# The perceiver stage's next batch of rows loaded from another DMA queue, and one value projection a step earlier

## The reference

```python
xn = layernorm(x, ln_x_g, ln_x_b)
ln = layernorm(latents, ln_l_g, ln_l_b)
q = ln @ Wq
kv_input = jnp.concatenate((xn, ln), axis=1)
kv = kv_input @ Wkv
k, v = jnp.split(kv, 2, axis=-1)
...
sim = jnp.einsum('bhid,bhjd->bhij', q, k)
sim = jnp.where(mask_full[:, None, None, :], sim, max_neg)
attn = softmax(sim)
out = jnp.einsum('bhij,bhjd->bhid', attn, v)
```

## Time and profile before

| | |
|---|---|
| median of 3 runs | 3383.18 us (3382.89 to 3386.95) |
| the profiled execution, own time | 3382.07 us |
| its span | 3380.3 us |
| PE busy | 3005.5 us, 89% of the span |
| VectorE busy | 2083.6 us, 62% |
| ScalarE busy | 1558.0 us, 46% |
| GpSimd busy | 1327.4 us, 39% |
| mean granted clock of PE | 0.934 |
| moved by DMA | 220.43 MB, mean 65 GB/s |

### The profile page before, as it was taken

One profiled execution on the slowest core, in us unless ns is written; L12 is line 12 of the kernel. 1 busy time (PEld: TensorE's weight loads), 2 busy tenths in 40 slices (PEclk: granted clock), 3 DMA queues, 4 the chain that ended last, 5 costly groups with the idle time before them and its releaser, 6 DMA issues. The chain is left out here.

```text
span 3380.3 us, 44846 instructions
## 1 busy us (share of the span) xinstructions
PE 3005.5 (89%) x16620; PEld 2534.8 (75%) x16620; DVE 2083.6 (62%) x4123; ACT 1558.0 (46%) x3036; POOL 1327.4 (39%) x913
## 2 busy tenths in 40 slices
PE   6888999968664999999999999999999769999998
PEld 5677777744433898989899898989989657777777
DVE  4766666622365776767777676777767654444432
ACT  2333333311033676767667676766767522222222
POOL 1444444410021465656556565655656530111110
PEclk9899999977765999999999999999999979999999
DMA  5112121112078112121211112111121231111100
GB/s 178 36 46 60 48 61 39 48 66 95 3 267 318 46 34 61 36 61 37 62 37 34 59 37 62 37 59 35 36 62 37 79 127 35 68 50 50 50 25 25
DMA packets 131551, 220.43 MB, mean 65 GB/s; under 512 B 44750, under 2 KB 46799, under 8 KB 127246
## 3 DMA queue, kind: packets, MB, share of 16 engines
q1 hardware_dynamic: 117933, 168.09, 16.4%
q10 hardware_dynamic: 13408, 49.56, 4.0%
HBM read 112.01 MB, written 69.47 MB: 54 GB/s over the span
## 5 line engine op out<-in xcount | busy, mean ns | idle before, releaser
L1635 POOL TENSOR_SCALAR pa_Pr<-pa_Pr,pa_rs 128x590 f32<-128x590 f32 x512 | 904.6, 1771 | 699.9 <-DVE pa_rs L1864 699.9
L1868 DVE TENSOR_REDUCE pa_least<-pa_S 128x1 f32<-128x590 f32 x512 | 391.3, 764 | 242.3 <-PE pa_S L1699 240.4
L1764 ACT ACTIVATE pa_PTh<-pa_W 128x512 fp32r<-128x512 f32 (+1 forms) x640 | 367.7, 596 | 174.4 <-PE pa_W L1710 158.5
L1819 DVE TENSOR_TENSOR pa_PTl<-pa_W,pa_PTh 128x512 fp32r<-128x512 f32 (+1 forms) x640 | 422.0, 683 | 33.2 <-ACT pa_PTh L1764 25.4
L1796 ACT ACTIVATE pa_Pr<-pa_S,pa_least 128x590 f32<-128x590 f32 x512 | 385.2, 752 | 79.3 <-DVE pa_least L1868 76.2
L1710 PE MATMUL pa_W<-pa_ident,pa_Pr 128*128 128x128 f32 (+1 forms) x2560 | 368.7, 275 | 9.7 <-DVE pa_Ql L1834 8.9
L1710 PEld LDWEIGHTS pa_W<-pa_ident,pa_Pr 128*128 128x128 f32 (+1 forms) x2560 | 306.8, 143 | 34.0 <-DVE pa_Ql L1834 12.0
L1724 PE MATMUL pa_O<-pa_PTh,pa_V 128*128 128x512 f32 (+1 forms) x640 | 293.2, 458 | 11.6 <-DVE pa_PTl L1819 8.1
L1697 PE MATMUL pa_S<-pa_U,pa_Qh 128*128 128x296 f32 (+1 forms) x1024 | 234.1, 311 | 44.7 <-DMA pa_Um<-pa_U 44.4
L1725 PE MATMUL pa_O<-pa_PTl,pa_V 128*128 128x512 f32 (+1 forms) x640 | 257.8, 403 | 0.0
L1697 PEld LDWEIGHTS pa_S<-pa_U,pa_Qh 128*128 128x128 f32 x1024 | 180.3, 195 | 71.1 <-DMA pa_Um<-pa_U 47.7
(11 more groups left out here) (400 smaller groups left out, 7223.2 us busy)
## 6 DMA issues: line engine op xcount, KB each, us to landing
pa_Um<-pa_U SPq DMA_DIRECT2D x128, 147.5 KB
pa_Qh<-pa_Qh SPq DMA_DIRECT2D x128, 128.0 KB
o_s<-pa_O_pair SPq DMA_DIRECT2D x64, 256.0 KB, 2.6
ex_o_raw<-o_s SPq DMA_DIRECT2D x8, 2048.0 KB, 10.8
z_s<-la_z_hi ACTq DMA_DIRECT2D x8, 1180.0 KB, 7.6
z_s<-la_z_lo ACTq DMA_DIRECT2D x8, 1180.0 KB, 10.0
pa_z_hi<-z_s ACTq DMA_DIRECT2D x8, 1180.0 KB, 6.0
pa_z_lo<-z_s ACTq DMA_DIRECT2D x8, 1180.0 KB, 10.1
```

The lines of the kernel that those rows point to most:

```text
L1635: pool.tensor_scalar(p, p, rs[:, g % 2, t:t + 1], None, ALU.mult).then_inc(*pool_s.mark("probs", n))
L1764: act.activation(out, src, ACT.Copy, scale=scale).then_inc(*act_s.mark("hi", *name))
L1819: dve.tensor_tensor(out, src, f32(hi_ap), ALU.subtract).then_inc(*dve_s.mark(*name))
L1868: dve.tensor_reduce(least[:, g % 2, t:t + 1], scored[n % 2], AX, ALU.min).then_inc(*dve_s.mark("least", n))
```

## The change

The loads of `z` move from ScalarE's queue to SyncE's. For batch 0 they are issued between the second and the third slab of weights (`w_sync` is split); for a next batch right behind the two key copies of the last pair, ahead of the output store, and SyncE waits for the last keys' matmuls first (they are the last readers of the rows in `z`). ScalarE issues none. And for the first quad of a batch, the last value projection (j = 4) comes at tick 16 instead of 17.

```diff
--- before.py
+++ after.py
@@ -1551,7 +1551,7 @@
         for q in range(QUADS):
             base = 2 * LEAD * (q - 1)
             for j, (tick, early) in enumerate(((6, True), (7, False), (14, True), (14, False), (15, False)) if q % BQ else
-                                              ((13, True), (13, False), (14, False), (15, False), (17, False))):
+                                              ((13, True), (13, False), (14, False), (15, False), (16, False))):
                 v_at.setdefault((base + tick, early), []).append((q, j))
         v_unit = lambda q, j: ("V", q, j // 2 * 2)
         v_last = lambda j: j % 2 or j == NC - 1
@@ -1585,7 +1585,13 @@
         @block.sync
         def _(sp):
             sp.dma_start(mask_words[:, :], a["mask_BxS2_bk0"]).then_inc(mask_in, 16)
-            w_sync(sp)
+            def load(b):
+                for n in range(2):
+                    sp.dma_start(f32(z[n][:, :, :]), z_s[n][b:b + 1].rearrange("b p c z -> p (b c) z")).then_inc(z_in, 16)
+
+            w_sync(sp, 0, 2)
+            load(0)
+            w_sync(sp, 2)
             sp.wait_ge(mask_row, 1)
 
             def store(p):
@@ -1607,6 +1613,9 @@
                     r = slice(x * HD, (x + 1) * HD)
                     sp.wait_ge(*act_s.after("hi", "K", p, 1, x))
                     sp.dma_start(f32(Um[m][x][r, :]), f32(U[m][x][r, :])).then_inc(dup[m], 16)
+                if p % BP == BP - 1 and p + 1 < PAIRS:
+                    sp.wait_ge(*pe_s.after("K", p, 1))
+                    load(p // BP + 1)
                 if p >= 2:
                     store(p - 2)
             for p in range(PAIRS - 2, PAIRS):
@@ -1756,10 +1765,6 @@
 
         @block.scalar
         def _(act):
-            def load(b):
-                for n in range(2):
-                    act.dma_start(f32(z[n][:, :, :]), z_s[n][b:b + 1].rearrange("b p c z -> p (b c) z")).then_inc(z_in, 16)
-
             def copy(out, src, *name, scale=1.0):
                 act.activation(out, src, ACT.Copy, scale=scale).then_inc(*act_s.mark("hi", *name))
 
@@ -1787,7 +1792,6 @@
                         act.wait_ge(*pe_s.after("PV", *divmod(g * NC + c - RING, NC)))
                     copy(PTh[0:KEYS[c], ring(g, c), :], bank_of[u][0:KEYS[c], :], *u)
 
-            load(0)
             w_scalar(act, 0, FIRST)
             for n in range(1 - LEAD, STEPS + 2 * NT + 1):
                 g, t = divmod(n, NT)
@@ -1797,8 +1801,6 @@
                                    bias=least[:, g % 2, t:t + 1], accum_out=rs[:, g % 2, t:t + 1]).then_inc(*act_s.mark("exp", n))
                 for u in evacuated(n - 1):
                     read(u)
-                    if u[0] == "K" and u[2] == 1 and u[1] % BP == BP - 1 and u[1] + 1 < PAIRS:
-                        load(u[1] // BP + 1)
                 if n in (-4, -3, -2):
                     w_scalar(act, n + 7, n + 8)
                 if t == 0 and head(g - 2):
```

## The result

| | before | after |
|---|---|---|
| median | 3383.38 us (4 runs, 3382.89 to 3386.95) | 3327.14 us (4 runs, 3322.43 to 3332.2) |
| ratio, 95% interval | | 0.9832 (0.9814 to 0.985) |
| the profiled execution, own time / span | 3382.07 / 3380.3 us | 3332.2 / 3330.4 us |
| mean granted clock | 0.934 | 0.938 |

The change takes 56 us off; the forecast was 57, to 3325.

A forecast was written before the change was run, and what follows sets the result against it. PE's work was taken to set the perceiver stage's pace, so any PE idle time removed is gained. 48 + 5 + 4 = 57 us off 3382 gave 3325 us, range 3311 to 3346.

The forecast's parts named there:

- the three places: Batch changes, last value unit and stage's start, forecast to take 48, 5 and 4 us off, 57 in all.
- The copies before z: At seven batch changes, key copies issued ahead of z end PE's wait: 6.9 us each, 48 us (37 to 58).
- the rival that it is mostly clock: At the batch changes, from the experiments' theories: the first part's gain is mostly clock; no size or chance given.
- the clock too high: From scores to query at a batch change: 7.15 us against 4.26 at full clock, so low clock costs 2.9 us.
- the rival of the falling clock: At the batch changes the clock falls all the same: 2.9 us seven times, 20 us; 3345 us, chance 0.11.
- the first term: At seven batch changes: key copies issued before z, 48 us off (37 to 58).
- The value unit: Last value unit one step earlier, seven times: 0.6 us new wait for 1.28, 5 us off (0 to 8.9).
- The start: Stage's start: first weight slabs go before z, third slab is cut earlier; 4 us off (0 to 5.5).
- The store behind z: At batch changes VectorE's O write waits about 2 us longer; cost 0, without cover up to 10 us in all.
- Turns between the queues: At batch changes, packets of z still get among the copies', PE waits as before: 9 us left, 3373 us, chance 0.05.
- A queue that works off its DMAs one after the other: SyncE's queue at batch changes and start: each transfer waits for the one ahead; slower, 3398 us, chance 0.04.
- the rival asked for 2 us more: At the batch changes z comes 2 us later, the query waits, 14 us given back: 3339 us, chance 0.07.

The follow-up runs named there:

- e4: Kernel before with ScalarE still issuing the next batch's z loads, but later, behind SyncE's key copies: 3340.61 us against 3384.68, ratio 0.9869.
- e9: Changed kernel with the next batch's two z loads issued ahead of the key copies in SyncE's queue: 3371.18 us against 3382.7 for the kernel before, ratio 0.996.
- e6: Changed kernel run again, nothing altered: 3327.93 us against 3382.86 for the kernel before, ratio 0.9837.
- e12: Changed kernel with z loads in halves and each batch change's output store issued from ScalarE's queue: 3320.52 us against 3382.7 for the kernel before, ratio 0.9815.
- e10: Changed kernel with z loads issued later, after the scores that open the next pair: 3369.24 us against 3382.7 for the kernel before, ratio 0.996.
- e1: Kernel before with only the last value projection moved from tick 17 to 16: 3375.8 us against 3384.68, ratio 0.997.
- e11: Changed kernel with each batch change's output store issued from ScalarE's queue, just ahead of the copies: 3326.1 us against 3382.7 for the kernel before, ratio 0.9832.
- e7: Changed kernel with each z load cut in two halves, each with its own semaphore: 3323.15 us against 3382.86 for the kernel before, ratio 0.9824.
- e8: Changed kernel with each z load cut in four pieces of one chunk: 3336.57 us against 3382.86 for the kernel before, ratio 0.9858.
- e5: Changed kernel with the output store issued ahead of the two z loads in SyncE's queue: 3351.74 us against 3382.86 for the kernel before, ratio 0.9911.

## Why the prediction was right

The measured total is nearer to the forecast than its parts are: the three places give 54.5 us of 57 in the profiled executions; the nearly 2 us that the medians' 56 have beyond that are no more than scatter.

*The copies before z: forecast 48 us, measured 45.5.* The mechanism held in each step: the copies' wait went seven times of eight, PE ran on to the query, and a wait for z took its place (forecast 1.4 us each, measured 1.3). The interval was to be 22.5 us and is 22.9 on average. The forecast put the query 9.98 us behind the copies' issue (1280.1 - 1270.12), the first change has 10.67. PE was ready after 1279.11 - 1.71 - 1268.44 = 8.96 us, forecast 8.58. The pair e4 and e9 shows that order alone does this.

*How it divides.* The sums over the seven intervals across a change, before and in e6 (us in all, busy us of each engine, means):

```profile
sum 206.03, PE 160.74 PEld 141.85 DVE 123.62 ACT 111.37 POOL 98.91; mean PE 22.96 PEld 20.26 DVE 17.66 ACT 15.91 POOL 14.13
sum 157.92, PE 143.67 PEld 125.59 DVE 120.77 ACT 112.36 POOL 98.66; mean PE 20.52 PEld 17.94 DVE 17.25 ACT 16.05 POOL 14.09
```

PE's busy time falls by 17.1 us and its idle time by 31.0. So the gain is mostly idle time, and the rival that it is mostly clock fails. The forecast had put the clock too high, at 2.9 us a change; it is 2.4. What was off is the way from the scores to the query at full clock, which it had by subtraction as 4.26 us. In e12, where nothing interrupts it, it is 4.56:

```profile
1269.45 0.44 PE L1708 MATMUL pa_S<-pa_U,pa_Qh 128*128 128x296 f32 x2
...
1274.01 0.48 PE L119 MATMUL pa_W<-pa_z_hi,pa_Wq_hi 128*128 128x512 f32 x1
```

The copies' wait made up for it: the forecast took the 5.42 us of the first change for all, and it is the shortest of the seven, whose mean is 5.6; and the new wait is 1.1 us on average in e6, not 1.4. That the three errors cancel to 48.1 against 48 is luck.

*That the clock stays up was right, with one exception.* It does at six changes of seven (at all in e6). At the seventh the rival of the falling clock came true. PE's query and the windows of the changed kernel there:

```profile
2423.29 0.50 PE L119 MATMUL pa_W<-pa_z_hi,pa_Wq_hi 128*128 128x512 f32 x1 [2.30 <-DMA pa_z_lo<-z_s]
```

```profile
2424.00:2427.00 3.00, 3.00 (x9) 2.32 (x8) 2.69 (x6) 0.84 (x2) 1.97 (x2) 0.50 0.00 0
2427.00:2429.00 2.00, 2.00 (x13) 1.77 (x13) 0.51 (x1) 1.04 (x2) 1.56 (x1) 0.92 0.00 0
```

Behind the longest query wait, 2.30 us, the clock is 0.50 from about 2423.9 to 2427.3. This interval is 25.25 us, 2.7 more than the mean of the other six; 1.2 of that is the longer wait (2.3 against 1.1), 1.5 the clock. The Trainium skill ("TensorE: Matmul & The Clock Gate", the terms at its start) prices this stretch of 3.4 us at its length times a half, 1.7; the rows give 1.5 and nearly agree. For the stretch of 6.8 us in the kernel before they don't: the rule gives 3.4, the runs 2.4. The miss of 2.5 us in the first term is this one change: e6, without it, has 48.1 us (206.03 - 157.92). That idle time brings a loss of clock with it is shown by e10, where 26 us of it cost 41.

*The value unit: forecast 5 us, measured 4.1.* The waits went as forecast, 1.28 us each gone; the new wait was sized at 0.6 and is 0.3. By the waits that would be 8.9 - 2.2 = 6.7 us. The intervals give 4.1, in e1 as after. Most of the other 2.6 us are no wait at all: by the windows of the seven intervals PE's busy time for the same matmuls goes up from 187.93 us to 190.06, by 2.1, at a granted clock of 1.00 in both. The forecast didn't have this. That its sum came near is partly luck, two errors against each other: the bank's release was worked out 0.3 us too late, and the longer busy time was not foreseen.

*The start: forecast 4 us, measured 4.1 in the wait,* 4.9 up to the second pair's copies. One step of it was off: the third slab was to be cut some 16.7 us after the stage's first DMA issue (1083.9 against 1067.20), and is cut after 17.4 (1087.79 - 1070.37), where it was 21.0 before; ScalarE's row of the changed kernel:

```profile
1087.79 1.91 ACT L156 ACTIVATE pa_Wkv_hi<-pa_Pr 128x2048 fp32r<-128x2048 f32 x1 [6.56 <-DMA pa_Pr<-L_xattn_Wkv]
```

*The store behind z: forecast about 2 us of waiting for VectorE, cost 0.* It waits longer than that, and PE doesn't feel it. VectorE's total, and the first of the seven:

```profile
DVE pa_O_pair L1855 <- DMA o_s<-pa_O_pair: 22.0, 7, 4.2
```

```profile
1279.81 0.68 DVE L1855 TENSOR_TENSOR pa_O_pair<-pa_O,pa_low 64x512 f32<-64x512 f32 x1 [3.54 <-DMA o_s<-pa_O_pair]
```

3.1 us each on average. PE has the query from 1279.11, and e11 shows the cover: without this wait the kernel is no faster. The cover has an edge. The forecast priced its lack at up to 1.5 us each; with PE some 1 us earlier VectorE's lateness costs 0.5 (e7), and with the store later 1.5 (e8).

*The rivals.* Turns between the queues would have left the copies' wait as it was; it is gone, in either queue. The Trainium skill says that a DMA engine takes turns between queues packet by packet ("DMA: Bandwidth & Descriptors", Queues, rings and completion order). Taken alone it would lead one to expect small copies to get through; in the kernel before they were reported complete only when the whole 2.36 MB had moved, of which another queue had issued the second half only 0.06 us ahead, and the measurement decides. It decides about the time that counts for PE; whether the engines took turns in between, no row shows. A queue that works off its DMAs one after the other would have made it slower than before; z_lo lands 8.4 us after its issue, sooner than before. At the first change z was 0.7 us later than forecast; over all seven its wait was no longer than forecast, where the rival asked for 2 us more.

## What to carry to other kernels

When a small transfer that is soon needed and a bulk load come due together, it was the order of issue that decided here, whichever queues they were in: a bulk load ahead held the small one for its whole length, one issued half a microsecond behind it did not. Put the bulk load directly behind, not later. Cutting it where its reader can begin with a part paid clearly only together with moving the store away; so count the issues that then stand ahead of whatever comes next in that queue. Don't carry the rule over to a store ahead of a load untried: e5 and e11 differ by 26 us. Idle time of PE can carry half clock behind it, so price a wait with both.

## What the runs showed of the hardware

- Copies issued right behind the two loads of z (2.36 MB), from the other queue or the same (e9), were usable 9.7 us after their issue; issued ahead of z, within 4.2 us.
- One 256 KB store to device memory directly ahead of the loads, in their queue, cost 24 us over seven changes: at each of them the last of z trickled in for 1 to 2 us behind the bulk (at the first at a DMA share of 0.15 to 0.04, e5). A store 1.6 us ahead of the loads, from the other queue, cost nothing (e11).
- Halving the loads gained 4.8 us by the medians and 1.4 by the traces (e7), quartering them lost 8.6 (e8); halves with the store moved to the other queue gained 9.4 at the changes (e12).
- The clock can fall behind a pause of 2.0 us (e11) or 2.3 (after) and be up behind pauses of 2.4 (e6) and 2.9 (e5); what decides between them isn't in these profiles. In e5, with pauses of 2.9 us on average, it fell five times of seven.
- The same matmuls in the intervals behind a change kept PE busy 187.93 us in one order and 190.06 in another, at a granted clock of 1.00 in both (before and after).
